# A tile of the attention stage is finished once, in the unit behind its last one

## The chip, the cores and the metric

The kernel runs on one core of one Trainium2 chip. The metric is the device time of one execution in microseconds (us); the time shown is a median of repeated runs. The engines are TensorE (PE, with its weight loads as PEld), VectorE (DVE), ScalarE (ACT), GpSimd (POOL) and SyncE (SP), each with its own instruction stream; they meet only at semaphores.

## What is computed

A graph network on 6250 nodes with 256 features and 100000 edges that are sorted by destination: three layers of mean aggregation with two products each, then one attention layer with 8 heads, two batch norms and a feed-forward part. Only the attention layer is touched. With `src` and `dst` extended by one loop edge per node it is

```
s = einsum('nhc,nhc->nh', Qh, Kh) / sqrt(HEAD_DIM)
alpha = leaky_relu(s[src] + s[dst], NEG_SLOPE)
m = segment_max(alpha, dst, num_segments=N)
e = exp(alpha - m[dst])
denom = segment_sum(e, dst, num_segments=N)
a = e / denom[dst]
msg = Vh[src] * a[:, :, None]
attn = segment_sum(msg, dst, num_segments=N).reshape(N, D_MODEL)
h = x + attn @ Wo + bo
h = _batch_norm(h, bn1_g, bn1_b)
h2 = relu(h @ W1 + b1) @ W2 + b2
h = _batch_norm(h + h2, bn2_g, bn2_b)
```

## The kernel before

Nodes lie in 49 tiles of 128 (`NT`). Edges lie in 196 blocks of 512 (`NB`, `BE`), and 14 blocks make a batch (`BB`), so that there are 14 batches (`KS`), counted here from 0. A block is four groups (`BJ`) of 128 edges.

In the attention stage four things run beside each other. POOL gathers the rows of V and s for every edge, four indirect DMAs per block, into a ring that holds two batches (L1010). SP refills index lists, windows of scores and marks, and gives ring slots free as PE has used them (L1073). PE, DVE and ACT work through the batches in turn, and each batch has two parts. `softmax(k)` turns the scores of the 14 blocks, finds the maxima by scans on DVE and makes the weights; it starts on ACT with L1254, which needs the batch's gathers, and on PE with L1137. In the midst of it the scores of batch k+1 are prepared. `weigh(k)` then sums the weighted rows by node tile.

A tile whose edges lie in two batches is worked on in both. A *unit* is one pair of batch and tile; there are `UNITS` = NT + KS - 1 = 62 of them, since the last tile of a batch is also the first of the next. A unit covers the blocks `b0` to `b1` that hold edges of its tile (read from `unit_table`, L972): about four or five in a full unit, fewer in the first and the last unit of a batch. Per block, DVE weights the gathered rows (L1499) and compares edge targets with the tile's node numbers to get one-hot rows (`src_onehots`, L1510, in two halves of two groups; one buffer holds the four groups, so a half is rewritten only when PE has used it), and PE multiplies both (L1212). At the end of the unit ACT copies the sums out of PSUM (L1312).

Every unit also takes an earlier tile some steps further: DVE's `attention` makes the mean from the sums of the unit before (L1480 to L1494), PE's `turn` transposes that mean (L1178), PE's `products` multiplies by Wo and adds the node's own row (L1188, L1189), ACT copies both out (L1290, L1297), stores the result to `hc_dram` (L1299) and loads the next own row (L1284) and the next V rows (L1309). Which tile a unit stores is read from the table `out_tile`. A tile that lies in two batches passes through all of this twice, the first time with incomplete sums; its second store replaces the first.

The sums of a tile that goes on into the next batch are carried: ACT zeroes `carry` after every unit (L1313), and behind a batch's softmax DVE writes into it the old sums, scaled to the new maximum (`carry_over`, L1461 and L1462). PE starts every unit's sums with `carry` times the identity (L1206), so it adds the carried sums in a batch's first unit and zeros in the others.

The order of the work is the order of the code of each engine; nothing is scheduled by a planner. Loops over units and blocks are loops at run time (L1196, L1207 on PE; L1512, L1523 on DVE), and the batches are written out one behind the other.

Of the kernel before, what the change touches and what calls it, by code (L numbers as in the profile page):

```python
# [17 lines left out]
P = 128  # L18
# [21 lines left out]
def gnn_kernel(nc, x, src, dst, sage_w, sage_b, Wq, bq, Wk, bk, Wv, bv, Wo, bo, W1, b1, W2, b2,  # L40
# [19 lines left out]
    OUTS = UNITS + 3  # L60
# [15 lines left out]
    hln_dram = dram("hln_dram", (NT, P, D))  # L76
    vs_table = dram("vs_table", (NP, VS))
    hc_dram = dram("hc_dram", (P, NT, KD * P))
# [6 lines left out]
    with ExitStack() as ctx:  # L85
# [99 lines left out]
        out_tile = sb("out_tile", [1, OUTS], I32)  # L185
# [206 lines left out]
        def batch_tables_vector(dve):  # L392
# [41 lines left out]
            def per_batch(a):  # L434
# [7 lines left out]

            unit_no = blocks_c[0:1, SLOTS - 3:SLOTS - 3 + OUTS]
            before = unit_f[0:1].rearrange("a i k t -> a (i k t)")[:, 0:OUTS * (KS - 1)].rearrange("a (u k) -> a u k", k=KS - 1)
            link(dve.tensor_tensor(joined[:, 0:KS - 1], batch_f[:, 2:KS + 1], blocks_c[0:1, SLOTS + 1:SLOTS + KS], ALU.add))
            link(dve.tensor_tensor(before, joined[:, 0:KS - 1].rearrange("a (u k) -> a u k", u=1).broadcast_to([1, OUTS, KS - 1]),
                                   unit_no.rearrange("a (u k) -> a u k", k=1).broadcast_to([1, OUTS, KS - 1]), ALU.is_le))
            link(dve.tensor_reduce(joined[:, KS:KS + OUTS], before, AX.X, ALU.add))
            link(dve.tensor_tensor(joined[:, KS:KS + OUTS], unit_no, joined[:, KS:KS + OUTS], ALU.subtract))
            link(dve.tensor_scalar(out_tile[:], joined[:, KS:KS + OUTS], 0.0, None, ALU.max))  # L450

# [10 lines left out]
        TABLES = 39  # L462
# [445 lines left out]
        def project_vector(dve, t):  # L908
# [26 lines left out]
            "edge_placed", "own_placed", "carry_made", "carry_zero",  # L935
# [39 lines left out]
        def tile_out(eng, u):  # L975

            return eng.value_load(out_tile[0:1, bass.ds(u, 1)], min_val=0, max_val=NT - 1)

# [12 lines left out]

        def stored_through(sp, t):

            both = sp.value_load(tile_span[0:1, t:t + 1], min_val=0, max_val=NB * NB - 1)
            return (both // (NB * BB) + (t + 5)) * 16

# [17 lines left out]
        def attend_sync(sp):  # L1014
# [33 lines left out]
            sp.wait_ge(G["tail_out"], 48)  # L1048
# [27 lines left out]
        def attend_tensor(pe):  # L1076
# [15 lines left out]
            def dst_scores(k, c, t_before):  # L1092
# [5 lines left out]
                if t_before is not None:  # L1098
                    u = t_before + (k - 2)
                    pe.wait_ge(G[("agg_taken", "lhs_made", "h_made")[c]], (u + 2) * (KD if c == 2 else 1))  # L1100
# [73 lines left out]
            def turn(u):  # L1174
                pe.wait_ge(G["attn_made"], u + 1)
                pe.wait_ge(G["lhs_made"], u + 1)
# [4 lines left out]
            def products(u):  # L1181
                pe.wait_ge(G["hln_in"], (u + 1) * 16)
                pe.wait_ge(G["h_made"], (u + 1) * KD)
# [8 lines left out]
            def weigh(k):  # L1192
                t0, t1 = tiles_of_batch(pe, k)
                if k + 1 < KS:
                    pe.wait_ge(G["dst_taken"], len(CHUNKS) * (k + 2))
                with pe.Fori(t0, t1 + 1) as t:  # L1196
                    u = t + k
                    b0, b1 = unit(pe, k, t)
                    turn(u)
                    products(u)  # L1200
                    pe.wait_ge(G["own_placed"], k + 1)
                    if k > 0:
                        pe.wait_ge(G["carry_made"], k)
                    pe.wait_ge(G["carry_zero"], u + 1)
                    apart(pe)
# [582 lines left out]
```

## Time and profile before

| | us |
|---|---|
| median of 3 runs (4452.23 to 4456.71) | 4455.09 |
| the profiled execution: its time | 4452.3 |
| its span, first to last instruction | 4450.5 |
| POOL's gathers of the attention stage | 3087.9 to 4103.1 |
| PE busy in the whole span | 3593.5 (81%) |
| POOL busy | 3017.0 (68%) |
| DVE busy | 2129.4 (48%) |
| ACT busy | 510.3 (11%) |

The times are positions in one execution, in us from the start of the span. An engine that is busy all the time need not be the bound, and one that idles can be: what counts in a stage is whose next instruction waits for whom. In the rows an idle stretch ahead of an instruction stands in brackets with what ended it; "issue" is time in which the engine waited for nothing that the profile shows, so mostly for its own branches, loads of registers and semaphore steps. An f32 matmul leaves two records in the trace (so a block, four of them, is `x8`), a transpose one.

### The profile page before, as it was taken

How to read it: one execution, taken by the hardware profiler on the slowest of the kernel's cores; microseconds unless marked ns; L12 is line 12 of the kernel's file. 1: busy time of each engine (PE TensorE's matmuls, PEld its weight loads, DVE VectorE, ACT ScalarE, POOL GpSimd, SP SyncE). 2: the span in 40 equal slices, each digit the busy share in tenths (PEclk: the TensorE clock that was granted, in tenths of full speed). 3: DMA queues.
4: the chain of work that ended last, by engine and by line, in shares of the span. 5: the costliest groups of instructions: out<-in, count | busy, mean ns of one | idle time of the engine just before them, and what ended most of it. 6: DMA issues, size and time to landing. Idle time of an engine off the chain costs nothing. (4 is left out here: it accounts for less than half of the span.)

```text
span 4450.5 us, 81354 instructions
## 1 busy us (share of the span) xinstructions
PE 3593.5 (81%) x16118; PEld 2489.4 (56%) x16119; DVE 2129.4 (48%) x6179; ACT 510.3 (11%) x1179; POOL 3017.0 (68%) x3154
## 2 busy tenths in 40 slices
PE   4888888897888888887888888895578787877787
PEld 2565655565565565564566666663356555655534
DVE  4333333334333333332455555453477777777733
ACT  2000000000000000000001010010121112111122
POOL 4777777776777777776777777774777777776000
PEclk9999999998999999998999999998779888888899
DMA  6333333334333333333444444445555555554211
GB/s 206 105 115 115 115 105 114 115 105 117 105 115 114 115 105 114 114 105 102 125 131 129 133 129 132 128 133 116 153 163 151 161 152 159 153 156 135 76 67 58
DMA packets 279618, 549.72 MB, mean 124 GB/s; under 512 B 103278, under 2 KB 172854, under 8 KB 275646
## 3 DMA queue, kind: packets, MB, share of 16 engines
q0 software_dynamic: 150528, 414.45, 32.7%
q10 hardware_dynamic: 66142, 75.48, 5.1%
q1 hardware_dynamic: 62848, 58.74, 4.3%
q8 instruction: 28, 0.46, 0.0%
q14 instruction: 72, 0.59, 0.0%
HBM read 490.73 MB, written 56.88 MB: 123 GB/s over the span
## 5 line engine op out<-in xcount | busy, mean ns | idle before, releaser
L587 POOL DMA_INDIRECT arena<-h_table,idx_v x2352 | 2236.8, 951 | 798.9 <-issue 714.9
L694 PE MATMUL banks<-arena 128*128 x5856 | 1466.8, 395 | 283.5 <-SPq L609 255.5
L694 PEld LDWEIGHTS banks<-arena 128*128 128x128 f32 x5856 | 1108.1, 195 | 604.1 <-issue 415.1
L646 DVE TENSOR_SCALAR arena<-iota_t,dst_e 128x128 f32<-128x128 f32 x2928 | 851.5, 309 | 839.0 <-PE banks L694 560.0
L1010 POOL DMA_INDIRECT arena<-vs_table,idx_v x784 | 776.7, 991 | 286.7 <-issue 283.4
L697 PE MATMUL banks<-zeros 128*128 128x512 bf16 x2440 | 661.7, 386 | 0.0
L1212 PE MATMUL banks<-arena 128*128 x1952 | 504.4, 403 | 46.6 <-DVE arena L1510 45.7
L1212 PEld LDWEIGHTS banks<-arena 128*128 128x128 f32 x1952 | 358.4, 191 | 185.4 <-issue 120.1
L744 DVE TENSOR_SCALAR small<-banks 128x1 f32<-128x1 f32 x147 | 23.3, 158 | 738.7 <-PE banks L698 738.7
L697 PEld LDWEIGHTS banks<-zeros 128*128 128x128 bf16 x2440 | 244.0, 100 | 235.1 <-issue 19.5
L798 ACT ACTIVATE lhs<-banks 128x512 f32<-128x512 f32 x147 | 87.8, 597 | 2356.7 <-PE banks L708 1651.5
L717 PE MATMUL banks<-arena,lhs 128*128 128x256 f32 x1176 | 293.1, 392 | 6.1
L717 PEld LDWEIGHTS banks<-arena,lhs 128*128 128x128 f32 x1176 | 211.3, 189 | 84.6 <-ACT lhs L798 45.5
L1499 DVE TENSOR_TENSOR arena<-arena,banks (+1 forms) x196 | 239.4, 1221 | 28.4 <-issue 11.8
L1510 DVE TENSOR_TENSOR arena<-iota_t,dst_e 128x256 f32<-128x256 f32 x488 | 196.3, 423 | 54.0 <-PE banks L1212 39.6
L893 PE MATMUL banks<-arena 128*128 128x512 f32 x196 | 98.5, 626 | 54.5 <-ACT arena L901 50.6
L634 DVE TENSOR_SCALAR iota_t<-iota_n,tile_base 128x128 f32<-128x128 f32 x147 | 50.6, 344 | 157.4 <-issue 156.5
L708 PE MATMUL banks<-ident,tiles 128*128 128x128 f32 x294 | 62.1, 293 | 78.1 <-DVE tiles L749 78.1
L1188 PE MATMUL banks<-lhs,arena 128*128 128x128 f32 x520 | 97.5, 318 | 10.9 <-DMA tiles<-hln_dram 10.9
L714 PE MATMUL banks<-arena,ones_row 1*128 1x256 f32 x294 | 102.1, 426 | 0.0
L1633 PE MATMUL banks<-arena 128*128 (+2 forms) x208 | 88.2, 579 | 15.6 <-DVE arena L1592 15.6
L1188 PEld LDWEIGHTS banks<-lhs,arena 128*128 128x128 f32 x520 | 81.8, 224 | 18.0 <-issue 12.6
(240 smaller groups left out, 2407.0 us busy)
## 6 DMA issues: line engine op xcount, KB each, us to landing
arena<-h_table,idx_v POOLq DMA_INDIRECT x2352
arena<-dst_dram SPq DMA_DIRECT2D x14, 1792.0 KB
arena<-vs_table,idx_v POOLq DMA_INDIRECT x784
h_table<-arena ACTq DMA_DIRECT2D x12, 1024.0 KB
hc_dram<-lhs ACTq DMA_DIRECT2D x65, 128.0 KB
tiles<-hln_dram ACTq DMA_DIRECT2D x64, 128.0 KB
tiles<-vs_table ACTq DMA_DIRECT2D x63, 128.0 KB
vs_table<-arena ACTq DMA_DIRECT2D x49, 132.0 KB
```

The source lines that it names most:

```text
L587: pool.indirect_dma_start(ring[:, s * BJ + j, 0:width], None, table, bass.IndirectOffsetOnAxis(idx_v[:, half, n * BJ + j:n * BJ + j + 1], ...
L646: dve.tensor_scalar(onehot[:, j, :], iota_t[:], dst_e[:, bass.ds(b * BJ + j, 1)], None, ALU.is_equal).then_inc(W["onehot_made"], 1)
L694: pe.matmul(agg[:, 0:D + 1], onehot[:, j, :], ring[:, (b % SLOTS) * BJ + j, 0:D + 1], start=False, stop=False).then_inc(W["onehot_used"], 1)
L697: pe.matmul(idle_ps, zeros[:, 0:P], zeros[:], start=True, stop=True)
L714: pe.matmul(dense[:, 0:D], ones_row[:], b_sage[0:1, l, :], start=True, stop=False)
L717: last = pe.matmul(dense[:, 0:D], lhs[:, k, :], w_sage[:, l, k, :], start=False, stop=k == 2 * KD - 1)
L893: pe.matmul(qk_ps, lhs_q[:, k, :], w_qkv[:, k, 0:2 * D], start=k == 0, stop=k == KD - 1)
L1010: pool.indirect_dma_start(v_ring[:, at, 0:VS], None, vs_table, bass.IndirectOffsetOnAxis(idx_v[:, half, s * BJ + j:s * BJ + j + 1], 0)).th ...
L1188: pe.matmul(dense[:, fs], w_o[:, i, fs], lhs[:, i, :], start=i == 0, stop=False)
L1212: pe.matmul(agg[:, 0:RW], onehot_v[:, j, :], v_ring[:, (b - (k - k % 2) * BB) * BJ + j, :], start=False, stop=False).then_inc(G["a_used"], 1)
L1499: dve.tensor_tensor(v, v, w.broadcast_to([P, BJ, HEADS, C]), ALU.mult).then_inc(G["rows_ready"], 1)
L1510: dve.tensor_tensor(onehot_v[:, j:j + 2, :], nodes_twice, ends_of(b * BJ + j), ALU.is_equal).then_inc(G["a_made"], 2)
```

## The change

A tile passes through `attention`, `turn`, `products`, copy and store once, in the unit behind its last one. The units are split in the code: the first unit of a batch stands by itself ahead of the loop, starts from `carry`, sums its blocks and does nothing for earlier tiles; the loop runs over the batch's other tiles, and each of these units starts its sums with a bf16 product of zeros and finishes an earlier tile. ACT's zeroing of `carry` and the table `out_tile` with its five DVE steps are gone; the loads and stores are addressed by the tile's own number with a fixed shift of two and three places, for which `hln_dram` and `hc_dram` get more rows (one of them is written with zeros at the start of the stage). The node numbers are moved to the next tile in the loop alone, and the one-hot rows of a batch's first block are made at the start of its softmax instead of at the start of its first unit. The cut diff:

```diff
-    OUTS = UNITS + 3
+    LOADS_BEHIND, STORES_BEHIND = 2, 3
...
-            act.dma_start(hln_dram[t], hln).then_inc(Q["hln_out"], 16)
+            act.dma_start(hln_dram[bass.ds(t + LOADS_BEHIND, 1)].rearrange("o p d -> p (o d)"), hln).then_inc(Q["hln_out"], 16)
...
             def weigh(k):
                 t0, t1 = tiles_of_batch(pe, k)
-                if k + 1 < KS:
-                    pe.wait_ge(G["dst_taken"], len(CHUNKS) * (k + 2))
-                with pe.Fori(t0, t1 + 1) as t:
-                    u = t + k
-                    b0, b1 = unit(pe, k, t)
-                    turn(u)
-                    products(u)
-                    pe.wait_ge(G["own_placed"], k + 1)
-                    if k > 0:
-                        pe.wait_ge(G["carry_made"], k)
-                    pe.wait_ge(G["carry_zero"], u + 1)
-                    apart(pe)
-                    pe.matmul(agg[:, 0:RW], ident[:], carry, start=True, stop=False)
+
+                def sums_of(t, b0, b1):
                     with pe.Fori(b0, b1 + 1) as b:
                         pe.wait_ge(G["rows_ready"], b + 1)
                         for j in range(BJ):
                             pe.matmul(agg[:, 0:RW], onehot_v[:, j, :], v_ring[:, (b - (k - k % 2) * BB) * BJ + j, :],
                                       start=False, stop=False).then_inc(G["a_used"], 1)
                     pe.matmul(agg[:, 0:RW], zeros[:, 0:P], zeros[:, 0:RW], start=False, stop=True).then_inc(G["agg_done"], 1)
+
+                _, b1 = unit(pe, k, t0)
+                if k + 1 < KS:
+                    pe.wait_ge(G["dst_taken"], len(CHUNKS) * (k + 2))
+                pe.wait_ge(G["own_placed"], k + 1)
+                if k > 0:
+                    pe.wait_ge(G["carry_made"], k)
+                pe.matmul(agg[:, 0:RW], ident[:], carry, start=True, stop=False)
+                sums_of(t0, k * BB, b1)
+                with pe.If(t1 > t0):
+                    with pe.Fori(t0 + 1, t1 + 1) as t:
+                        b0, b1 = unit(pe, k, t)
+                        turn(t)
+                        products(t)
+                        pe.wait_ge(G["agg_taken"], t + (k + 1))
+                        apart(pe)
+                        pe.matmul(agg[:, 0:RW], zeros[:, 0:P], zeros[:, 0:RW], start=True, stop=False)
+                        sums_of(t, b0, b1)
                 return t1
 
...
             def weigh(k):
                 t0, t1 = tiles_of_batch(act, k)
-                with act.Fori(t0, t1 + 1) as t:
-                    u = t + k
-                    take_turned(u)
-                    take_out(u, tile_out(act, u))
-                    own_load(u, tile_out(act, u + 1))
-                    act.wait_ge(G["attn_made"], u + 2)
-                    act.dma_start(x_tile.rearrange("p (o d) -> p o d", o=1), v_rows[:, bass.ds(t, 1), 0:D]).then_inc(G["v_in"], 16)
-                    act.wait_ge(G["agg_done"], u + 1)
+
+                def take_sums(t):
+                    act.wait_ge(G["agg_done"], t + (k + 1))
                     apart(act)
                     act.activation(sums, agg[:, 0:RW], ACT.Copy).then_inc(G["agg_taken"], 1)
-                    act.activation(carry, zeros[:, 0:RW], ACT.Copy).then_inc(G["carry_zero"], 1)
+
+                take_sums(t0)
+                with act.If(t1 > t0):
+                    with act.Fori(t0 + 1, t1 + 1) as t:
+                        take_turned(t)
+                        take_out(t)
+                        own_load(t)
+                        act.wait_ge(G["attn_made"], t + 1)
+                        act.dma_start(x_tile.rearrange("p (o d) -> p o d", o=1), v_rows[:, bass.ds(t, 1), 0:D]).then_inc(G["v_in"], 16)
+                        take_sums(t)
 
...
                 if more:
                     dst_onehots(k + 1, 0)
                     dst_onehots(k + 1, 1)
+                src_onehots(tiles[0], k * BB)
                 dve.wait_ge(keep_in[k % 2], (k // 2 + 1) * 16)
                 dve.wait_ge(G["rows_in"], k + 1)
...
-                with dve.Fori(t0, t1 + 1) as t:
-                    u = t + k
-                    b0, b1 = unit(dve, k, t)
-                    dve.wait_ge(G["a_made"], (b0 + t) * BJ + 1)
-                    apart(dve)
-                    dve.tensor_scalar(iota_t[:], iota_n[:], tile_base[:, bass.ds(t, 1)], None, ALU.add).then_inc(G["base_moved"], 1)
-                    dve.wait_ge(G["base_moved"], u + 1)
-                    apart(dve)
-                    src_onehots(t, b0)
-                    attention(u)
+                def pairs(t, b0, b1):
                     with dve.If(b0 < b1):
                         with dve.Fori(b0 + 1, b1 + 1) as b:
                             weighted(b, b - (k - k % 2) * BB, b - k * BB)
                             src_onehots(t, b)
 
+                _, b1 = unit(dve, k, t0)
+                pairs(t0, k * BB, b1)
+                with dve.If(t1 > t0):
+                    with dve.Fori(t0 + 1, t1 + 1) as t:
+                        b0, b1 = unit(dve, k, t)
+                        dve.wait_ge(G["a_made"], (b0 + t) * BJ + 1)
+                        apart(dve)
+                        dve.tensor_scalar(iota_t[:], iota_n[:], tile_base[:, bass.ds(t, 1)], None, ALU.add).then_inc(G["base_moved"], 1)
+                        dve.wait_ge(G["base_moved"], t + 1)
+                        apart(dve)
+                        src_onehots(t, b0)
+                        attention(t, k)
+                        pairs(t, b0, b1)
+
...
+            act.dma_start(hln_dram[1], zeros[:].bitcast(F32)).then_inc(G["tail_out"], 16)
```

On DVE, between the scaling of the carried sums and the first work on a block, the kernel before has this (L1462 is the last step of the carry, L1517 moves the tile's node numbers, L1510 makes the one-hot rows):

```order
L1462 TENSOR_TENSOR arena<-arena,banks 128x16
L1512 UNCONDITIONAL_BRANCH
L1512 ISA
L972 TENSOR_LOAD unit_table
L972 ISA x2
L1515 ISA
L1517 ISA
L1517 TENSOR_SCALAR iota_t<-iota_n,tile_base 128x128
L1518 REGISTER_ALU
L1509 REGISTER_ALU
L1510 ISA
L1510 TENSOR_TENSOR arena<-iota_t,dst_e 128x256
```

and after it stand the second L1510, the seven steps of `attention` (L1480 to L1494) and only then L1499, the weighting of block two. In the changed kernel (its lines are about 10 lower at the top and differ by less here: L1458 is the carry, L1494 the weighting, L1499 the one-hot rows) the same place reads:

```order
L1458 TENSOR_TENSOR arena<-arena,banks 128x16
L962 ISA
L962 TENSOR_LOAD unit_table
L962 ISA x2
L1508 REGISTER_ALU
L1508 COMPARE_AND_BRANCH
L1509 UNCONDITIONAL_BRANCH
L1509 ISA
L1494 ISA
L1494 TENSOR_TENSOR arena<-arena,banks 128x4x256
```

The move of the node numbers is gone from the first unit, `attention` is gone from it, and the first pair-making of the unit has moved away; the weighting of block two follows the carry.

Where it went: DVE at the start of a batch's softmax, before (L1369 are compares of the next batch, L1409 the first scan) and then in the changed kernel:

```order
L963 TENSOR_LOAD batch_t
L963 ISA x2
L1369 TENSOR_SCALAR arena<-arena,node_id 128x2560 x2
L1409 SCALAR_TENSOR_TENSOR arena<-arena 112x512
L1410 SCALAR_TENSOR_TENSOR arena<-arena 112x512
```

```order
L953 TENSOR_LOAD batch_t
L953 ISA x2
L1364 TENSOR_SCALAR arena<-arena,node_id 128x2560 x2
L1498 ISA
L1499 TENSOR_TENSOR arena<-iota_t,dst_e 128x256
L1498 REGISTER_ALU
L1499 TENSOR_TENSOR arena<-iota_t,dst_e 128x256
L1405 SCALAR_TENSOR_TENSOR arena<-arena 112x512
```

The one-hot rows of the batch's first block are now made ahead of the first scan.

On PE, the head of a batch's first unit before (L1178 and L1188, L1189 turn and multiply the earlier tiles, L1206 adds the carry to the sums):

```order
L972 TENSOR_LOAD unit_table
L972 ISA x2
L1175 REGISTER_ALU
L1178 MATMUL banks<-ident,tiles 128x128 [waits g_lhs_made,g_attn_made]
L1178 MATMUL banks<-ident,tiles 128x128
L1182 REGISTER_ALU
L1183 REGISTER_ALU [waits g_hln_in]
L1188 MATMUL banks<-lhs,arena 128x128 [waits g_h_made]
L1188 MATMUL banks<-lhs,arena 128x128
L1189 MATMUL banks<-ident,tiles 128x128
L1188 MATMUL banks<-lhs,arena 128x128 x2
L1189 MATMUL banks<-ident,tiles 128x128
```

with L1206 next, and in the changed kernel (L1190 adds the carry, L1180 multiplies a block):

```order
L962 ISA
L962 TENSOR_LOAD unit_table
L962 ISA x2
L1190 MATMUL banks<-arena,ident 128x272 [waits g_carry_made,g_own_placed,g_dst_taken]
L1175 UNCONDITIONAL_BRANCH
L1175 ISA
L1179 ISA [waits g_rows_ready]
L1180 ISA [waits g_a_made]
L1180 MATMUL banks<-arena 128x272
```

The turning and the six products are gone from the first unit; the addition of the carry now stands first and waits on DVE's carry directly.

## Rows read from the trace of the kernel before

**Rows 1.** One line of the code: the gathers, L1010, with what they waited for.

```profile
L1010 POOL DMA_INDIRECT arena<-vs_table,idx_v x784: 940/946/1930, 3087.9 to 4102.2; - x196
...
  SPq L1073: 3.4, 11
```

**Rows 2.** Timeline of POOL: start us, us, engine line op [idle before <-releaser].

```profile
3087.86 0.94 POOL L1010 DMA_INDIRECT arena<-vs_table,idx_v  x1 [48.18 <-issue]
...
3230.02 1.40 POOL L1010 DMA_INDIRECT arena<-vs_table,idx_v  x1 [0.30 <-issue]
...
3244.39 1.92 POOL L1010 DMA_INDIRECT arena<-vs_table,idx_v  x1 [0.30 <-issue]
...
4102.19 0.94 POOL L1010 DMA_INDIRECT arena<-vs_table,idx_v  x1 [0.30 <-issue]
```

**Rows 3.** Timeline of ACT: the first operation of a batch's softmax.

```profile
3233.24 0.39 ACT L1254 ACTIVATE arena<-arena 128x224 f32<-128x224 f32 x1 [2.23 <-DMA arena<-vs_table,idx_v]
...
3311.42 0.66 ACT L1254 ACTIVATE arena<-arena 128x224 f32<-128x224 f32 x2
...
3383.86 0.66 ACT L1254 ACTIVATE arena<-arena 128x224 f32<-128x224 f32 x2
...
4059.47 0.66 ACT L1254 ACTIVATE arena<-arena 128x224 f32<-128x224 f32 x2
...
4138.74 0.66 ACT L1254 ACTIVATE arena<-arena 128x224 f32<-128x224 f32 x2
```

**Rows 4.** Timeline of DVE, batch 9: from the carried sums to block two.

```profile
3857.25 0.17 DVE L1462 TENSOR_TENSOR arena<-arena,banks 128x16 f32<-128x16 f32 x1
3858.82 0.32 DVE L1517 TENSOR_SCALAR iota_t<-iota_n,tile_base 128x128 f32<-128x128 f32 x1 [1.40 <-issue]
...
3861.80 0.42 DVE L1494 TENSOR_TENSOR tiles<-tiles,small 128x256 f32<-128x256 f32 x1 [0.23 <-DVE tiles L1490]
3862.41 1.22 DVE L1499 TENSOR_TENSOR arena<-arena,banks  x1 [0.19 <-issue]
3863.55 0.75 DVE L1510 TENSOR_TENSOR arena<-iota_t,dst_e 128x256 f32<-128x256 f32 x2
```

**Rows 5.** Timeline of PE, the same stretch of batch 9.

```profile
3857.13 0.66 PE L1178 MATMUL banks<-ident,tiles 128*128 128x128 f32 x2 [0.58 <-issue]
...
3860.17 0.78 PE L1206 MATMUL banks<-arena,ident 128*128 128x272 f32 x2
3860.79 2.00 PE L1212 MATMUL banks<-arena 128*128 x8
3864.14 2.10 PE L1212 MATMUL banks<-arena 128*128 x8 [1.36 <-DVE arena L1510]
```

**Rows 6.** Timeline of PE, the first unit of batch 13.

```profile
4158.27 0.66 PE L1178 MATMUL banks<-ident,tiles 128*128 128x128 f32 x2
...
4161.28 1.11 PE L1206 MATMUL banks<-arena,ident 128*128 128x272 f32 x2
4162.19 3.03 PE L1212 MATMUL banks<-arena 128*128 x8
4165.82 2.10 PE L1212 MATMUL banks<-arena 128*128 x8 [0.60 <-DVE arena L1510]
```

**Rows 7.** Timeline of PE, the second unit of batch 12.

```profile
4087.19 0.38 PE L1178 MATMUL banks<-ident,tiles 128*128 128x128 f32 x2
4090.47 0.68 PE L1188 MATMUL banks<-lhs,arena 128*128 128x128 f32 x4 [2.90 <-DMA tiles<-hln_dram]
```

**Rows 8.** Timeline of DVE, the start of batch 9's softmax.

```profile
3834.79 1.68 DVE L1369 TENSOR_SCALAR arena<-arena,node_id 128x2560 bf16<-128x2560 int16 x2 [1.32 <-issue]
3838.10 1.30 DVE L1409 TENSOR_TENSOR_SCAN arena<-arena 112x512 f32<-112x512 bf16 x1 [1.63 <-issue]
```

**Rows 9.** One line of the code: the block loop L1207 on PE's queue.

```profile
L1207 PEldq COMPARE_BRANCH  x244: 67/208/234, 3183.0 to 4208.1; - x122
```

**Rows 10.** Timeline of SP's queue: the loads of the stored tiles.

```profile
4138.76 90.74 SPq L1702 DMA_DIRECT2D arena<-hc_dram  x7
```

More of the change, by code:

```diff
@@ L460, in batch_tables_vector @@
             assert step[0] == TABLES
-        TABLES = 39
+        TABLES = 34
         def batch_tables_scalar(act):
@@ L1223, in attend_tensor @@
                 t_before = weigh(k)
-            for u in (UNITS, UNITS + 1):
-                turn(u)
-                products(u)
-            pe.wait_ge(G["lhs_made"], UNITS + 3)
-            products(UNITS + 2)
+            for t in (NT, NT + 1):
+                turn(t)
+                products(t)
+            pe.wait_ge(G["lhs_made"], NT + 2)
+            products(NT + 2)
         def attend_scalar(act):
@@ L1240, in attend_scalar @@
             act.dma_start(x_tile[:], v_rows[:, 0, 0:D]).then_inc(G["v_in"], 16)
-            for n, count in (("agg_taken", 1), ("carry_zero", 1), ("lhs_made", 1), ("h_made", KD), ("stored", 16), ("hln_in", 16)):
+            for n, count in (("agg_taken", 1), ("lhs_made", 1), ("h_made", KD), ("stored", 16), ("hln_in", 16)):
                 act.sem_inc(G[n], count)
@@ L1318, in attend_scalar @@
                 weigh(k)
[L1319 to L1323 removed]
+            for t in (NT, NT + 1):
+                take_turned(t)
+                take_out(t)
+                own_load(t)
+            take_out(NT + 2)
         SPLIT_DONE = 12
         SPLITS_MADE = 5
+        STEPS = 6
         def attend_vector(dve):
@@ L1351, in attend_vector @@
             dve.sem_inc(G["a_made"], 1)
+            dve.sem_inc(G["step"], STEPS)
+            dve.tensor_scalar(iota_t[:], iota_n[:], tile_base[:, 0:1], None, ALU.add).then_inc(G["base_moved"], 1)
+            dve.wait_ge(G["base_moved"], 1)
             chain = [0]
@@ L1499, in weighted, with src_onehots @@
                 dve.tensor_tensor(v, v, w.broadcast_to([P, BJ, HEADS, C]), ALU.mult).then_inc(G["rows_ready"], 1)
+            def src_onehots(t, b):
+                for j in range(0, BJ, 2):
+                    dve.wait_ge(G["a_used"], (b + t) * BJ + (j + 2))
+                    dve.tensor_tensor(onehot_v[:, j:j + 2, :], nodes_twice, ends_of(b * BJ + j), ALU.is_equal).then_inc(G["a_made"], 2)
             def weigh(k, t0, t1):
@@ L1530, in attend_vector @@
                 weigh(k, *softmax(k))
-            attention(UNITS)
+            attention(NT, KS - 1)
         def tile_stats(dve, t, done):
@@ L1699, in feed_forward_sync @@
             for g in range(NT // GO):
-                sp.wait_ge(G["stored"], stored_through(sp, (g + 1) * GO - 1))
-                apart(sp)
+                sp.wait_ge(G["stored"], ((g + 1) * GO + STORES_BEHIND) * 16)
                 sp.dma_start(h_cols[:, g * GO:(g + 1) * GO].rearrange("p t f n -> p t (f n)"),
-                             hc_dram[:, g * GO:(g + 1) * GO, :]).then_inc(h_back[g], 16)
+                             hc_dram[:, g * GO + STORES_BEHIND:(g + 1) * GO + STORES_BEHIND, :]).then_inc(h_back[g], 16)
             sp.wait_ge(G["a_used"], BJ + BJ * PAIRS)
```

87 lines of the change are left out of this document (31 added, 56 removed).

## The prediction, written before the changed kernel ran

> **What bounds the kernel now.** I read first which engine is never kept waiting in the stage that the change touches, then the starts of the batches, then one first unit on each engine.
>
> POOL: 784 gathers from 3087.9 us on, which waited for free ring slots 3.4 us in all [rows 1]. The reader is to see that ring and index loads never hold the gathers back. From the last gather of batch 1 (ends 3230.02 + 1.40 = 3231.4) to the last one of batch 13 (ends 4103.1) [rows 2] lie 12 batches in 871.7 us, 72.6 us each. That is the floor of this stage.
>
> The other engines: batch 1's softmax waited for its gathers and started at 3233.24, 1.8 us after the last of them; batches 2 and 3 start at 3311.42 and 3383.86, batches 12 and 13 at 4059.47 and 4138.74, with no wait for a gather in the row [rows 3]. So the chain softmax, weigh, softmax takes (4138.74 - 3233.24) / 12 = 75.5 us a batch, 78.2 and 72.4 by turns, and is 2.9 us slower than the gathers. It falls behind steadily: batch 13's gathers are usable at about 4103.1 + 1.8 = 4104.9, and its softmax (second conversion, 0.3 us after the first) runs at 4139.0, 34 us later. From batch 1 to the end the stage is bound by the chain of PE, DVE and ACT, not by POOL. What is saved per batch adds up until these 34 us are used up; then the gathers bind.
>
> **The change, part by part.**
>
> The first unit. Before, DVE ends the carry at 3857.42, sits 1.40 us, moves the node numbers, makes four one-hot groups and runs `attention` to 3862.22; block two is weighted from 3862.41 and its one-hot rows follow at 3863.55 [rows 4]. PE turns and multiplies from 3857.13, adds the carry at 3860.17, does block one from 3860.79 in 2.0 us, then waits 1.36 us for DVE and starts block two at 3864.14 [rows 5]. DVE's path sets that: 3864.14 - 3857.42 = 6.7 us from carry to block two.
>
> On DVE the changed kernel needs the idle stretch (1.4), a weighting (1.22), one half of the one-hot rows (0.4) and a hand-over of 0.2: 3.2 us, so 3.5 us less. But now PE is late next. Its carry product can start only about 0.2 us behind the carry, and it falls into the stretch in which PE's clock is at the lower of its two levels, 1.2 GHz, after the thin work of the softmax: the carry product's two records take 1.11 us in batch 13 against 0.78 in batch 9, where the clock rose in its midst [rows 5, 6]. In batch 13 the first L1212 starts 0.91 us behind L1206, and block one takes 3.03 us instead of 2.0 [rows 6]. With 0.25 us a record at 2.4 GHz (2.00 / 8) that is 5.4 records at 0.44 us, and the rise lies near 4164.6. A block wholly at the lower level is 8 x 0.44 = 3.5 us. Before, the turning and the products took the slow stretch, beside DVE's `attention`, where they cost nothing; now carry and blocks take it.
>
> When does it rise? 4164.6 - 4158.27 = 6.3 us after PE's steady work began in batch 13, and 3860.8 - 3857.13 = 3.7 us in batch 9 [rows 5, 6]. I take the middle, r = 5.0 us, and keep both ends. Carry and two blocks are 0.9 + 3.5 + 3.5 = 7.9 us at the lower level; behind the rise they take 0.57 of it (0.25 / 0.44). From the carry to the end of block two: 0.2 + r + (7.9 - r) x 0.57 = 4.7 + 0.43 r, which is 6.9 us for r = 5.0 (6.3 to 7.4). Before it was 6.7 + 2.0 = 8.7. Saved: 1.8 us (1.3 to 2.4). DVE stays ahead enough: its halves wait for PE's use of block one.
>
> The step between first unit and loop now has one more compare and branch on each engine. PE's take 0.2 us each [rows 9]; I charge 0.1 and keep 0 to 1.4 (a whole loop entry, the idle of L1517 [rows 4]). That leaves 1.7 us per batch; the ends are 1.3 + 0.1 - 1.4, about 0, and 3.5, DVE's path alone.
>
> Batch 12 has a first unit of one block. There PE's second unit waited 2.90 us for the own row, which is loaded a unit ahead [rows 7]; now it is loaded long before. I take 3.2 us for this batch (2.9 alone to 2.9 + 1.7).
>
> One-hot rows at the start of softmax: two halves, 0.75 us [rows 4], in DVE's 1.63 us between L1369's end and L1409 [rows 8], which waits for ACT. Taken at nothing; without that cover 0.75 us a batch.
>
> Later units: the zero product replaces a f32 product (two records), and the wait is for one ACT copy instead of two. PE waits for DVE behind it anyway; nothing (0 to 0.3 us in 48 units). Five small DVE steps in the tables run beside the second layer's gathers: nothing. ACT's store of zeros at the start of the stage runs while all wait for the first gathers: nothing. The last three finishing steps behind the last unit are as many as before, and the last load of stored tiles waits for them as before [rows 10].
>
> At one place a page speaks against the change. POOL's gathers that meet dense DVE work are longer: 1.92 us at 3244.39 and 1.40 at 3230.02 where most take 0.94 [rows 2]; that excess is 72.6 - 56 x 1.25 = 2.6 us a batch. GPSIMD Engine Reference of the Trainium skill (section 1, Specifications) has the SBUF interfaces shared with VectorE, with contention from instructions of two SBUF inputs, which the moved compare is. By that rule the gathers would lengthen where the compare now stands and shorten where `attention` went; no run here shows either, and while the chain binds neither changes the sum.
>
> **The sum.** Batch 0's saving is lost, since batch 1 waits for gathers (2.23 us in [rows 3]). Batches 1 to 11: 11 x 1.7 = 18.7. Batch 12: 3.2. Batch 13's own first unit: 1.7. Together 23.6 us. The lag at batch 13 falls from 34 to 12 us, so the gathers do not bind there; nearest they come in batch 3, where the lag is near 2.6. Profiled execution: 4452.3 - 23.6 = 4428.7. The median of the runs shown is 2.8 us above it (4455.09): predicted 4431.5.
>
> **The rivals.**
>
> A, the gathers become the bound. If PE's clock rises early or falls later than I think, the saving is DVE's 3.5 us; then batches 1 to 12 save more than the 34 us and the lag stays near 3. Time: 4455.1 - (34 - 3) - 3.5, about 4421. For it: DVE's path is really that short; against it: the slow records in every first unit that I read. Chance 0.15.
>
> B, little comes through. Branches, register loads and the clock eat most: 0.5 us a batch, 12 x 0.5 + 2.9, about 9 us: 4446. For it: the 1.40 us idle for one loop entry, and the changed kernel has two of them a batch. Against: most is hidden behind blocks in work. Chance 0.17, half of it within 0.2%, which is 8.9 us and about what a measurement of this kernel can tell from no change.
>
> C, slower: the clock. PE gets less to do at the head of a batch, and if it then waits for DVE between blocks the clock could stay at the lower level through the first and second unit. A block then costs PE 3.5 instead of 2.1 us [rows 5]; over 7 blocks that is 9.8 us more a batch, less 1.7, some 100 us in 12 batches: 4555. It decides from r = 5.0 + 1.7 / 0.43 = 9 us on. Against it: at the lower level PE is slower than DVE, so it has no gaps, and the longest r that I read is 6.3. Chance 0.05.
>
> D, the change doesn't do what it says: the finishing moves instead of going. The stores to `hc_dram` tell: 62 + 3 before, 48 + 3 expected. The instruction rows show it gone from the first unit; chance 0.01.
>
> **How the numbers follow.** My forecast has 0.62. Its own range is 4425 to 4438 (r at its ends). The range reaches to A below and most of B above: 4418 to 4444. Faster by over 0.2%: 0.62 + 0.15 + half of B = 0.86; within: 0.09; slower: 0.05.
>
> **What would show it.** Gathers of unchanged length and end, near 4103. Batch starts 73.8 us apart in the mean instead of 75.5, and batch 13's softmax near 4117 without a wait. In the first unit, carry to block two's start about 5 us instead of 6.7, with L1212's records at 0.4 us and PE, not DVE, late. 51 stores to `hc_dram`. No 2.9 us wait in batch 12. The prediction is wrong if batch starts wait for gathers from batch 3 on (A), or if the idle ahead of DVE's weighting and of the loop's first unit is well over 1.4 us (B).

## The result, and the profile after

| | before | changed |
|---|---|---|
| median (us) | 4453.66 (4 runs, 4452.11 to 4456.71) | 4427.85 (4 runs, 4421.73 to 4430.02) |
| ratio, 95% interval | | 0.9939, 0.9922 to 0.9956 |
| profiled execution | 4452.3 | 4428.64 |
| its first gather of the stage to its end | 4450.5 - 3087.9 = 1362.6 | 4426.8 - 3091.9 = 1334.9 |
| stores to `hc_dram` | 65 | 51 |

Faster by 0.6%, 3.65 us from the predicted 4431.5. The sum made for the profiled execution was 4428.7, and it took 4428.64. The agreement is better than the working behind it, as the rows show. In the changed kernel L1241 is ACT's first operation of a softmax, L1458 the carry, L1190 the carry product, L1180 a block's product, L1494 the weighting, L1499 the one-hot rows, L1294 the copy of the sums.

The gathers, against [rows 1] (one line of the code, with what it waited for and who waited for it):

```profile
L990 POOL DMA_INDIRECT arena<-vs_table,idx_v x784: 942/946/1915, 3091.9 to 4112.8; - x196
...
  SPq L1053: 3.0, 10
who waited for it (us, times):
  ACT arena L1241: 50.2, 6
```

The reader is to see two things. The first gather starts 4.0 us later than before: the layers ahead of the stage ended later in this execution. Three executions of the same changed kernel began the stage at 3091.9, 3095.9 and 3092.0, two of the kernel before (one with fewer gathers) at 3087.9 and 3089.2, and variants of the changed kernel, which differ from it in the stage alone, at 3086.0 to 3093.6. This scatter is wider than the 4.0 us, so they are not shown to come from the change, and I compare the stage from the first gather to the end, not positions. And ACT waited for gathers six times where it had waited three times before: two of the six lie in batch 0, the others in batches 1, 5, 7 and 12.

The starts of the softmax, against [rows 3] (timeline of ACT, start us, us, idle before in brackets):

```profile
3237.34 0.39 ACT L1241 ACTIVATE arena<-arena 128x224 f32<-128x224 f32 x1 [4.68 <-DMA arena<-vs_table,idx_v]
...
3312.93 0.66 ACT L1241 ACTIVATE arena<-arena 128x224 f32<-128x224 f32 x2
...
3382.84 0.66 ACT L1241 ACTIVATE arena<-arena 128x224 f32<-128x224 f32 x2
...
3676.09 0.39 ACT L1241 ACTIVATE arena<-arena 128x224 f32<-128x224 f32 x1 [2.76 <-DMA arena<-vs_table,idx_v]
...
4043.64 0.39 ACT L1241 ACTIVATE arena<-arena 128x224 f32<-128x224 f32 x1 [4.66 <-DMA arena<-vs_table,idx_v]
...
4118.10 0.66 ACT L1241 ACTIVATE arena<-arena 128x224 f32<-128x224 f32 x2
```

Behind batch 1, batches 5 (0.44 us), 7 (2.76) and 12 (4.66) now wait for gathers, 7.9 us of idle time. The last gather ends at 4113.7, is usable 1.8 us later, and batch 13's second conversion runs at 4118.4: the 34 us lag has become 2.9.

The first unit of batch 9, against [rows 4, 5] (timeline, here PE and DVE in one):

```profile
3844.51 0.17 DVE L1458 TENSOR_TENSOR arena<-arena,banks 128x16 f32<-128x16 f32 x1
...
3844.89 1.24 PE L1190 MATMUL banks<-arena,ident 128*128 128x272 f32 x2 [1.08 <-DVEq L1460]
...
3845.93 6.14 PE L1180 MATMUL banks<-arena 128*128 x16
3846.09 1.22 DVE L1494 TENSOR_TENSOR arena<-arena,banks  x1 [1.41 <-issue]
...
3848.10 0.43 DVE L1499 TENSOR_TENSOR arena<-iota_t,dst_e 128x256 f32<-128x256 f32 x1 [0.79 <-PE banks L1180]
...
3849.91 0.42 DVE L1499 TENSOR_TENSOR arena<-iota_t,dst_e 128x256 f32<-128x256 f32 x1 [1.38 <-PE banks L1180]
```

The carry product starts 0.21 us behind the carry and takes 1.24 us; PE then runs two blocks without a gap, and now DVE waits for PE twice. Two blocks take 6.14 us. At the 0.44 and 0.25 us a record of the prediction that is 11 records at 1.2 GHz and 5 at 2.4: the rise lies 6.0 us behind the start of the carry product. The granted clock agrees (three stretches, with the busy times of PE, PEld, DVE, ACT and POOL; the third number from the end is the granted clock, 0.50 for 1.2 GHz and 1.00 for 2.4):

```profile
3842.00:3850.50 8.50, 7.42 (x21) 5.63 (x22) 3.89 (x6) 0.54 (x1) 6.37 (x8) 0.50 0.67 179
3850.50:3851.00 0.50, 0.50 (x4) 0.42 (x3) 0.00 (x0) 0.00 (x0) 0.50 (x1) 0.91 0.59 101
3851.00:3853.00 2.00, 2.00 (x13) 1.45 (x12) 0.75 (x3) 0.40 (x1) 1.39 (x3) 1.00 0.46 120
```

Batch 12, against [rows 7] (timeline of PE):

```profile
4067.05 2.99 PE L1180 MATMUL banks<-arena 128*128 x8
4069.87 0.28 PE L1182 MATMUL banks<-zeros 128*128 128x272 bf16 x1
4069.99 0.38 PE L1157 MATMUL banks<-ident,tiles 128*128 128x128 f32 x2
4070.21 0.61 PE L1167 MATMUL banks<-lhs,arena 128*128 128x128 f32 x4
```

The wait of 2.90 us for the own row is gone.

The stage can be split by instants that both kernels have in every batch: the starts of the softmax's two conversions (ACT's first two operations there), the end of the carry, the starts of the copies of the sums. Sums over batches 1 to 13, in us:

| stretch | before | changed | gain |
|---|---|---|---|
| softmax (second conversion to carry) | 278.05 | 278.01 | 0 |
| first unit (carry to the copy of its sums) | 139.27 | 112.97 | 26.3 |
| the other units (copy to copy) | 548.48 | 543.59 | 4.9 |
| last copy to the next softmax's first conversion, which never waited for gathers here (12) | 7.38 | 3.53 | 3.9 |

For batches 1 to 12 alone this is 32.9 us. The waits for gathers behind batch 1 took 8.2 back (by the starts of the second conversions), so that batch 1 to batch 13 takes 881.0 us for 905.8; from there to the end it is 308.4 for 311.5. 32.9 - 8.2 + 3.1 = 27.8 us, which is the stage's 27.7 within rounding; the later start of the stage took 4.0 of it. Of the 3.1 behind batch 13's conversion, 1.5 are its first unit.

The 4.9 us of the other units and the 3.9 behind them were not in the prediction. The last units of batches 1, 3, 5, 7 and 9 are one block long, and show where they arise: on ACT. Before (timeline of ACT, batch 1's last unit):

```profile
3307.05 0.38 ACT L1290 ACTIVATE lhs<-banks 128x256 f32<-128x256 f32 x1 [1.51 <-PE banks L1189]
3307.88 0.63 ACT L1297 ACTIVATE lhs<-banks,cols 128x128 f32<-128x128 f32 x2 [0.44 <-issue]
3308.66 0.37 ACTq L1299 DMA_DIRECT2D hc_dram<-lhs  x1
3309.80 0.35 ACTq L1284 DMA_DIRECT2D tiles<-hln_dram  x1
3310.32 0.35 ACTq L1309 DMA_DIRECT2D tiles<-vs_table  x1
3310.80 0.40 ACT L1312 ACTIVATE arena<-banks 128x272 f32<-128x272 f32 x1 [2.30 <-issue]
3311.10 0.42 ACT L1313 ACTIVATE arena<-zeros 128x272 f32<-128x272 bf16 x1
```

and the same unit of the changed kernel:

```profile
3309.99 0.38 ACT L1277 ACTIVATE lhs<-banks 128x256 f32<-128x256 f32 x1 [1.92 <-PE banks L1168]
3310.27 0.62 ACT L1284 ACTIVATE lhs<-banks,cols 128x128 f32<-128x128 f32 x2
3311.04 0.36 ACTq L1286 DMA_DIRECT2D hc_dram<-lhs  x1
3311.57 0.35 ACTq L1271 DMA_DIRECT2D tiles<-hln_dram  x1
3312.08 0.36 ACTq L1303 DMA_DIRECT2D tiles<-vs_table  x1
3312.64 0.40 ACT L1294 ACTIVATE arena<-banks 128x272 f32<-128x272 f32 x1 [1.75 <-PE banks L1182]
```

Before, ACT stood idle 0.44 us ahead of L1297 and 0.77 us between the store and the own-row load (now 0 and 0.17): the reads of `out_tile` (`tile_out`, two per unit). In a unit of four blocks that is hidden. In one of one block ACT ends last, also now: PE's L1182, which the row names, had ended at 3311.94, and the copy starts 0.20 us behind ACT's own last load. The unit took 5.97 us, now 4.97 (five such units, 5.0 us). The zeroing L1313 stood in the way of the next softmax for 0.3 us. Batch 12's second unit gave 1.4 us more, and the remaining units took 1.5 us longer in the sum.

### The profile page after: what moved, and what is told of

The parts are those of the page before. It is cut to its first block and busy times, and to the rows that moved or that the text cites. A ratio compares the mean times of both kernels' runs of the same rounds, so it can differ in the third digit from the quotient of the medians.

```text
span 4426.8 us, 78800 instructions
## 1 busy us (share of the span) xinstructions
PE 3502.1 (79%) x15164; PEld 2445.3 (55%) x15875; DVE 2102.0 (47%) x6063; ACT 470.9 (11%) x1074; POOL 3025.8 (68%) x3154
## 5 line engine op out<-in xcount | busy, mean ns | idle before, releaser
L684 PEld LDWEIGHTS banks<-arena 128*128 128x128 f32 x5856 | 1108.8, 195 | 607.4 <-issue 418.0
L990 POOL DMA_INDIRECT arena<-vs_table,idx_v x784 | 783.2, 999 | 287.2 <-issue 284.2
L1180 PE MATMUL banks<-arena 128*128 x1952 | 511.5, 415 | 58.8 <-DVE arena L1499 58.8
L687 PE MATMUL banks<-zeros 128*128 128x512 bf16 x1730 | 504.5, 387 | 40.5 <-issue 4.2
L1180 PEld LDWEIGHTS banks<-arena 128*128 128x128 f32 x1952 | 364.7, 198 | 193.0 <-issue 120.1
L1494 DVE TENSOR_TENSOR arena<-arena,banks (+1 forms) x196 | 239.0, 1220 | 34.4 <-issue 26.2
L1499 DVE TENSOR_TENSOR arena<-iota_t,dst_e 128x256 f32<-128x256 f32 x488 | 193.9, 422 | 85.0 <-PE banks L1180 69.4
L698 PEld LDWEIGHTS banks<-ident,tiles 128*128 128x128 f32 x294 | 32.2, 141 | 101.3 <-DVE tiles L739 101.3
L883 PEld LDWEIGHTS banks<-arena 128*128 128x128 f32 x196 | 33.6, 190 | 97.1 <-issue 95.6
```

What stands on the lines that cost most here:

```text
L684: pe.matmul(agg[:, 0:D + 1], onehot[:, j, :], ring[:, (b % SLOTS) * BJ + j, 0:D + 1], start=False, stop=False).then_inc(W["onehot_used"], 1)
L687: pe.matmul(idle_ps, zeros[:, 0:P], zeros[:], start=True, stop=True)
L698: last = pe.transpose(tp[:, k, :], mean[:, k * P:(k + 1) * P], ident[:])
L883: pe.matmul(qk_ps, lhs_q[:, k, :], w_qkv[:, k, 0:2 * D], start=k == 0, stop=k == KD - 1)
L990: pool.indirect_dma_start(v_ring[:, at, 0:VS], None, vs_table, bass.IndirectOffsetOnAxis(idx_v[:, half, s * BJ + j:s * BJ + j + 1], 0)).th ...
L1180: pe.matmul(agg[:, 0:RW], onehot_v[:, j, :], v_ring[:, (b - (k - k % 2) * BB) * BJ + j, :], start=False, stop=False).then_inc(G["a_used"], 1)
```

## The experiments

The kernels ran in three groups, each against the kernel before on its chip, whose medians were 4458.95 us (the changed kernel again, and experiments 1 to 3), 4454.51 (4 to 6 and 8) and 4461.58 (7, 9 and the last two). Times of different groups are compared by their ratios. A saving of a stretch is told as in the table above.

**The changed kernel again.**

> The changed kernel itself, beside the runs that follow. Both theories: about 0.994 of the kernel before (4427 us). Of the start of the first attention gather, which lay 4.1 us later in the one profile of the changed kernel (3091.9 against 3087.9): if the change causes it, it is late again by about 4 us; if it is scatter between executions, it lies elsewhere within some us.

4428.34 us (4425.78 to 4432.94), ratio 0.9932 (0.9919 to 0.9946). Stage 1335.2 us, first units 113.6, waits for gathers behind batch 1 9.1 us in five batches (2.8, 1.4, 0.5, 0.9, 3.5). So the split repeats, and which batches wait shifts.

**1. The one-hot rows back in the first unit.** In DVE's code:

```diff
-                src_onehots(tiles[0], k * BB)      # in the softmax
...
                 _, b1 = unit(dve, k, t0)
+                src_onehots(t0, k * BB)
                 pairs(t0, k * BB, b1)
```

> The changed kernel, but the one-hot rows of a batch's first block are made again behind the carry, at the head of the first unit, not in the softmax. Theory (VectorE's path is short and TensorE, slow at its lower clock, sets the first unit): TensorE's block one then starts about 1.4 + 0.4 us behind the carry instead of 1.2, and the second weighting some 0.8 us later, so 0.6 to 1.0 us a batch is lost, 5 to 10 us in all where the gathers do not bind: 4431 to 4437. Of the gathers: if the moved compare in the dense softmax is what made them longer (999 ns in the mean against 991), they are back near 991; if not, they stay near 999. Rival (the move is what brings most of the gain): over 15 us lost.

4431.25 us, 0.9938 (0.9924 to 0.9952). First units 121.3 us, 7.7 more than the 113.6 above; but no batch behind 1 waits for gathers any more, and the stage is 1335.6, as without the edit. The loss fell into the slack before the gathers. The gathers' mean stays at 998 ns (999 in the changed kernel): the place of this compare does not lengthen them.

**2. PE's work back in the first unit.**

```diff
                 _, b1 = unit(pe, k, t0)
...
+                for f in range(KD):
+                    pe.transpose(tp[:, f, :], ident[:], ident[:])
+                for f in range(KD):
+                    for i in range(KD + 1):
+                        pe.matmul(dense[:, f * P:(f + 1) * P], w_o[:, i % KD, f * P:(f + 1) * P], ident[:], start=True, stop=True)
```

> The changed kernel, but TensorE does two transposes and six 128-column f32 products of constants ahead of the carry in every first unit, as much work as the removed turning and products; their results go unused. Theory (that work had filled the stretch at the lower clock and cost nothing there): the clock rises at the same place, carry and blocks come later but faster, and at most 1 us a batch is lost: 4427 to 4438. Rival (the gain is TensorE's work gone): its 3.9 us a batch come back, limited by the 24.7 us that the chain gained: 4448 to 4455.

4429.68 us, 0.9936 (0.9922 to 0.995). First units 119.9 us, 6.3 more (0.5 a batch), stage 1333.5, no wait for gathers behind batch 1. PE's work is nearly free at that place, as expected, and not wholly.

**3. Three small steps of DVE back in the first unit.**

```diff
                 _, b1 = unit(dve, k, t0)
+                for _ in range(3):
+                    link(dve.tensor_tensor(f_row, l_row, l_row, ALU.add))
                 pairs(t0, k * BB, b1)
```

> The changed kernel, but VectorE does three 112x512 f32 operations (about 0.7 us each with a wait behind each, 2.5 us together) in every first unit between the carry and the weighting of block two, as long as the removed attention steps; their results go unused. Theory (VectorE's attention ahead of block two was what set the first unit before): block two starts 1.4 + 2.5 + 1.2 + 0.6 = 5.7 us behind the carry instead of about 4.6, at the higher clock in most batches, and its end moves from 7.0 to about 8 us: 0.8 to 1.3 us a batch, 4434 to 4442. Rival (TensorE's removed work made the gain): no loss, 4427.

4434.37 us, 0.9947 (0.9933 to 0.996). First units 123.3 us, 9.7 more, stage 1342.9. The three steps take about as long as `attention` did there. Here the slack does not cover the loss, in part because the gathers became longer too (the page's costliest groups, busy us and mean ns):

```profile
L990 POOL DMA_INDIRECT arena<-vs_table,idx_v x784 | 789.6, 1007 | 286.6 <-issue 283.2
```

against 783.2 and 999 in the changed kernel (784.8 and 1001 in its second execution). Batches 5 and 12 still wait (2.8 and 2.2 us).

**4. PE's clock kept up through the softmax.** PE fills its waits in the softmax with products of zeros into an unused bank, 50 a batch (two of the eight places):

```diff
+            def fill(n):
+                for _ in range(n):
+                    pe.matmul(banks[:, 4, :], zeros[:, 0:P], zeros[:, 0:512], start=True, stop=True)
...
+                pe.wait_ge(G["rows_in"], k + 1)
+                fill(7)
...
+                fill(4)
                 pe.wait_ge(G["own_placed"], k + 1)
```

> The changed kernel, but TensorE fills its waits in the softmax with bf16 products of zeros (512 columns, results unused), so that its clock stays at the higher level into the first unit. Theory (two blocks at the lower clock cost about 2 us a batch, but the gathers now stand close behind the chain): carry and two blocks end about 5.2 us behind the carry's last VectorE step instead of 7.0, yet only what the chain still lags behind the gathers comes through, some 3 us, and 2 to 3 us in batch 13 itself: 4420 to 4424, with waits for gathers at most batch starts. Rival (the lower clock costs nothing in the end): 4427, or slower if the fillers stand in the way of real products.

4420.78 us (4417.88 to 4423.82), 0.9927 (0.9913 to 0.994); granted clock 0.964 for 0.934. Softmax 271.0 us for 278.0, first units 105.5 for 113.0. Timeline of PE, batch 9 (L1112 are the zeros, L1203 the carry product, L1192 the blocks):

```profile
3835.91 1.89 PE L1112 MATMUL banks<-zeros 128*128 128x512 bf16 x4 [0.98 <-issue]
3837.59 1.11 PE L1203 MATMUL banks<-arena,ident 128*128 128x272 f32 x2
3838.50 4.36 PE L1192 MATMUL banks<-arena 128*128 x16
```

Two blocks in 4.36 us instead of 6.14, though the carry product is still slow. The clock was not kept up everywhere: in batch 9 the granted clock is 1.00 from 3831.8 to 3835.5, 0.50 from 3836.5 to 3839.0 and 1.00 again from 3839.5, and the four fillers ahead of the carry product delay it to 1.79 us behind the carry, where it was 0.21. So this first unit takes 7.3 us for 7.6. In the first units of six batches (1, 3, 4, 6, 11 and 13) the granted clock stays at 1.00 in the first 5 us behind the carry, and batch 1's takes 5.6 us for 6.9.

The softmax gained 7.0 us and the first units 7.5. Of these 14.5 us the stage shows 5.2 (1329.7): seven batches behind batch 1 wait for gathers, 17.7 us in all, against 8.2.

**5 and 6. Fewer gathers, before and after.** From batch 2 on the fourth gather of every block is left out, and with it a quarter of the gathered rows (their ring slots keep what they held); everything else runs as it did.

```diff
+            two_batches(0, BJ)
+            with pool.Fori(1, KS // 2) as k2:
+                two_batches(k2, BJ - 1)
```

> The kernel before, but from batch 2 on only three of the four gathers of a block are made (the fourth group keeps old rows), so POOL is far ahead. Theory (before, the chain alone bound batches 1 to 13): no change beyond the contention that goes, 4449 to 4455. Rival (the gathers had a hand in it): over 9 us faster.

> The changed kernel with the same three gathers of four from batch 2 on. Theory (the gathers now bind in some batches: waits of 0.5, 2.9 and 4.8 us in the profile): about 8 us less than the changed kernel, 4417 to 4421. Rival (the gathers do not bind): as the changed kernel, 4427.

The kernel before: 4450.52 us, 0.9991 (0.9982 to 1.0), stage 1361.8 for 1362.6. The changed kernel: 4419.04 us, 0.9918 (0.9905 to 0.9932), stage 1324.9, no wait for gathers behind batch 1. Fewer gathers were worth 0.8 us of stage before and are worth 7 to 10 now (1331.8 to 1335.2 in three executions). That shows the bound moving.

**7. ACT's zeroing back.**

```diff
                     act.activation(sums, agg[:, 0:RW], ACT.Copy).then_inc(G["agg_taken"], 1)
+                    act.activation(a_row[:, 0:RW], zeros[0:R, 0:RW], ACT.Copy)
```

> The changed kernel, in which ACT writes zeros (into a scratch row) behind every copy of the sums, as it zeroed the carry before. Theory: between the last sums copy of a batch and the first ACT operation of the next softmax come back about 0.3 us a batch (3.5 us in the sum over the batches against 7.4 before), and in part the last short unit of odd batches (1.0 us in six batches). About 3 to 5 us in the whole, of which half is hidden by the waits for gathers: stage 1336 to 1340, against 1334.9 to 1335.2 without it. Rival: the zeroing lies beside PE's work and the end of the batch was shortened by the loop's new form: then the sum stays at 3.5 us and the time at the changed kernel's.

4431.91 us, 0.9934 (0.9921 to 0.9948). The stretch behind the last copy is back at 7.40 us (7.38 before, 3.53 changed). The short last units are not: the other units take 542.6 us. So the zeroing costs 0.3 us a batch, all of it covered here by fewer waits for gathers (stage 1335.1, where I had expected 1336 to 1340), and the 1.0 us of the short units is not its work. That those are the reads of `out_tile` is argued from the rows above (0.44 and 0.60 us of idle time that went); no experiment tried it alone.

**8. The clock kept up and fewer gathers.** Experiments 4 and 6 in one; the same rows are left out.

> Both together, fillers in TensorE's waits and three gathers of four from batch 2 on: what the chain costs at the higher clock with no gather in its way. Theory: 2 us or more a batch below the run with thin gathers alone, 25 to 35 us: 4385 to 4395. Rival (the lower clock costs nothing): 4417 to 4421 as there.

4400.73 us (4393.06 to 4403.03), 0.9881 (0.9866 to 0.9896), stage 1302.0. That is 18.3 us below experiment 6, and 22.9 us of stage. Softmax and first units give 8.9 and 14.6 us (267.0 and 98.8 for 275.9 and 113.4), 23.5 together: with the gathers out of the way all of it arrives, where 5 of 14.5 us did in experiment 4. The direction was as expected, the size was not: 4385 to 4395 was too low.

**9. All four pieces back** (experiments 1, 2, 3 and 7 in one).

> The changed kernel with all four pieces of work put back into the first unit and behind the sums copy: the one-hot rows of block one behind the carry, two transposes and six f32 products on PE, three small steps on DVE, and ACT's zeros. Theory (the work of the first unit is what the change saves, and the waits for gathers cover the first 8 us of any loss): alone, each piece gave 6.3 to 9.7 us back in the first units; together 17 to 24 us, first units 131 to 137 us in the sum (139.3 before, 113.0 changed), waits for gathers in batch 1 alone, stage 1350 to 1358 (before 1362.6), time 4443 to 4451. Rival: the pieces lie beside each other and the gain comes from the loop's new form: then together no more than 12 us in the first units and 4430 to 4438.

4444.17 us (4441.66 to 4446.06), 0.9961 (0.9947 to 0.9974). First units 131.6 us, last copy to conversion 7.4, stage 1349.5, no wait for gathers behind batch 1. PE, batch 9 (timeline; L1188 and L1191 are the work put back, L1195 the carry product):

```profile
3855.47 0.68 PE L1188 MATMUL banks<-ident 128*128 128x128 f32 x2 [0.27 <-issue]
3855.94 2.77 PE L1191 MATMUL banks<-ident,arena 128*128 128x128 f32 x12
3858.50 0.81 PE L1195 MATMUL banks<-arena,ident 128*128 128x272 f32 x2
3859.15 2.00 PE L1180 MATMUL banks<-arena 128*128 x8
3862.64 2.10 PE L1180 MATMUL banks<-arena 128*128 x8 [1.50 <-DVE arena L1504]
```

This is [rows 5] again: the idle PE work takes the slow stretch, the blocks are fast, and PE waits for DVE. In the first units the pieces give back 18.6 us together, less than the 23.7 that three of them gave back alone: they lie in part beside each other. Of 27.7 us of stage, 14.6 are these four pieces, net of the waits for gathers that went. The other 13.1 were not put back: 5.6 in the other units and 7.7 in the first ones (0.1 to 0.9 each, batch 12 1.3), less small rests. Which edit brought the 7.7 is not shown; the move of the node numbers, for one, was not among the four pieces.

**The last two: experiment 4 against the changed kernel on one chip.**

> The changed kernel again, beside the others of this call, as their measure. Theory: stage (first gather to end) 1335 us, first units 113 us, six or so waits for gathers of 8 us behind batch 1, time 4425 to 4431. Rival to the stage as the steady measure: the stage's length scatters by more than 2 us between executions.

> The version in which PE fills its waits in the softmax with products of zeros, again, beside the changed kernel on one chip. Theory: it is truly faster than the changed kernel, by 5 to 8 us (the stage 1329.7 against 1335.2), since the clock is up at the first unit, but most of what it saves is taken by waits for gathers: 4418 to 4424. Rival: the difference seen first was scatter between chips: then the two medians lie within 3 us.

The changed kernel: 4431.23 us (4425.64 to 4432.26), 0.9932 (0.9918 to 0.9946), stage 1331.8. With the fillers: 4423.7 us (4421.21 to 4431.48), 0.9918 (0.9905 to 0.9932), stage 1330.2. The medians lie 7.5 us apart, as expected, but the intervals of the ratios overlap and the two profiled stages differ by 1.6 us. The fillers' stretches repeat (first units 105.4, softmax 269.0), and so do waits for gathers in most batches. They help by 2 to 8 us; more closely it is not settled. My expectation that one kernel's stage is steady within 2 us did not hold: 1334.9, 1335.2 and 1331.8. In this second execution, too, the granted clock stays at 1.00 in six of 13 first units alone: the fillers as they stand do not recover the whole price of the lower clock.

## Why the prediction was right, point by point

- **The bound before** ([rows 1 to 3]) was read rightly: the thinned gathers change almost nothing before (0.9991, 0.8 us of stage).
- **The first unit**: 2.0 us a batch (26.3 / 13) against 1.7. The mechanism is as told: PE late instead of DVE, blocks at 1.2 GHz, and the transposes, the products and `attention` no longer in the way; block two of batch 9 starts 4.9 us behind the carry, where about 5 was expected. Experiments 1 to 3 each give back 0.5 to 0.7 us a batch of it, and experiment 9 brings back the old picture on PE. Batch 9's rise came 6.0 us after PE's first work, inside the 3.7 to 6.3 taken, but batch 9 is an extreme: over the 13 first units the granted clock rises 3.2 to 5.9 us behind the carry, 4.7 in the mean. With the carry product 0.2 us behind the carry that is an r of 3.0 to 5.7, and 4.5 in the mean for the 5.0 taken, which by the prediction's 0.43 r is 0.2 of the 0.3 us (an estimate). Batches 5 and 11, where the rise comes at 3.2 us, took only 6.4 us from the carry to the copy, against 6.9 to 7.6 in the other first units of two blocks.
- **Batch 12**: its first two units take 4.2 us less (7.33 and 12.70 to 4.48 and 11.31) against 3.2; in the changed kernel's other two executions 3.3. I took the 2.90 us of the own row in full, and that is not shown: in experiment 9 that wait is gone as well, and the two units still take 18.4 us of the 20.0.
- **The step that failed**: "Later units ... nothing", and ACT's part in it. I had looked for what PE waits for and passed over ACT, which ends last only in a unit of one block and at the end of a batch. 1.0 us in five units (by the rows the reads of `out_tile`) and 0.3 us in twelve batches (the zeroing, experiment 7): 8.9 us together. The diff shows both deletions; asking, for each, which unit has no cover would have found them.
- **The gathers do not bind**: wrong, and rival A was right in part. The prediction's own sign of A, batch starts that wait for gathers, came in batches 5, 7 and 12. The chain saved 32.9 us over batches 1 to 12, more than the 31 that the lag allowed, and the gathers took 8.2 us back (6.5 to 9.1 in three executions). A's reason, though, did not hold: the first units saved 2.0 us, not DVE's 3.5. The lag went by ACT's part on top of the first units', and by the gathers themselves: their mean rose from 991 to 999 ns, 6.5 us in the stage, so that their end moved from 4103.1 to 4113.7 (4.0 us of it by the later start) where "unchanged length and end" was expected. 34 us less the 24.7 that came through and these 6.5 leave 2.8, the lag of 2.9 seen at batch 13.
- **The one-hot rows in the softmax**: free, 278.05 and 278.01 us. GPSIMD Engine Reference of the Trainium skill (section 1, Specifications), by which the moved compare might lengthen the gathers, is not borne out there (998 ns with it back in its old place), but with experiment 3's three steps, each a sum of two SBUF inputs, the mean was 1007 and in experiment 9 1008, in line with it. Three executions of the changed kernel have 997 to 1001.
- **C and D** did not come: PE has no gaps in the first two blocks, and there are 51 stores.
- **The sum**: predicted 21.9 us over batches 1 to 12 and 1.7 behind; it was 32.9, less 8.2, and 3.1 behind, less 4.0 of a later start. The 11.0 us too little are about 3.2 in the first units of batches 1 to 11, 1.0 in batch 12, and ACT's 8.9 less some 2 that the remaining units took longer. With the 1.4 behind batch 13 they cancel against the 12.2 us left out (waits for gathers and later start): that the sum came within 0.1 us is luck, since two of its terms are wrong. They are not independent either, since a chain that saves more meets the gathers earlier, and that kept the error small.

## What to carry to other kernels

When a chain is ahead of a floor by a known lag, add up its savings against that lag first: what you mis-size beyond it is cut off by the floor, and putting work back costs little until the slack is used (experiments 1 and 2). For every deletion, look for the shortest unit of the loop, not the typical one; an engine that is 11% busy can end last there. Work that is taken from under a slow stretch of PE's clock hands the slow stretch to the work behind it: of the 3.5 us by which DVE's path became shorter by the rows, 2.0 arrived.

## What the runs showed of the hardware

- 50 bf16 products of 512 columns a batch in PE's waits raised the granted clock from 0.934 to 0.964 and shortened two f32 blocks from 6.14 to 4.36 us in batch 9. In six of 13 first units the clock stayed at 1.00; in batch 9 it fell to 0.50 just behind the softmax all the same.
- After the same softmax work PE's clock rises at different places: 3.2 to 5.9 us behind the carry in the 13 first units of the changed kernel, so that first units of two blocks take 6.4 to 7.6 us.
- Gathers of the same kind have a mean that follows the kernel: 991 ns before (also with a quarter fewer of them), 995 to 1001 in the changed one and most of its variants, 1007 and 1008 with three two-input DVE steps more per batch. Why the changed kernel lies 8 ns above the one before, with less DVE work, stays open; it isn't the moved compare.
- Kernels that are alike up to this stage start it up to 10 us apart (3086.0 to 3095.9 in the changed kernel and its variants), and the changed kernel's three executions up to 4.0 us apart; the length of its stage holds within 3.4 us.
